# Sums of squares of queries and keys: squares as the moving operand of four column tiles, a row copy and a turn, and norms taken later in the slot

## The chip, the cores and the metric

One core of one Trainium2 chip runs the kernel. The metric is the time on the device of one launch, in microseconds (us), as the median of several runs. The kernel's own names for the engines are used beside the usual ones: PE (TensorE, matrix products), DVE (VectorE), ACT (ScalarE), POOL (GpSimd), SP (SyncE, which here only starts transfers).

## The reference

The input x is 16 sequences of 512 positions by 128 features. A gated linear attention with 8 heads of 128 is followed by a layer norm, a mixture of experts and a second layer norm. The part that matters here:

```python
def _l2norm(u, eps=1e-12):
    n = jnp.sqrt(jnp.sum(u * u, axis=-1, keepdims=True))
    return u / jnp.maximum(n, eps)
...
q = _l2norm((x @ Wq).reshape(Bb, Tt, H, DK))
k = _l2norm((x @ Wk).reshape(Bb, Tt, H, DK))
v = (x @ Wv).reshape(Bb, Tt, H, DV)
alpha = jax.nn.sigmoid(x @ Wg).reshape(Bb, Tt, H, DK)

def step(S, qkva):
    q_t, k_t, v_t, a_t = qkva
    S = a_t[..., None] * S + k_t[..., None] * v_t[:, :, None, :]
    o_t = jnp.einsum('bhkv,bhk->bhv', S, q_t)
    return (S, o_t)
```

So each query and each key of each head is divided by its own length. That length is a sum over the 128 features.

## The kernel before, in words

The attention runs in 64 slots: 16 sequences times 4 pairs of heads (`P` counts slots, `p` is the pair within a sequence, `par = p % 2` picks one of two sets of buffers). In slot `P` the engines do three things interleaved: the scores of slot P in levels (`scores(par, P, j)` for j = 1, 3, 4, 5, 6, 7; level 6 joins halves of 32 positions, and level 7 halves of 64), the projections and norms of slot P + 1, and the states and outputs of slot P - 1. 63 slots have a next slot. After the slots the experts run ("the second half" below); the change does not touch them.

Queries and keys lie transposed: features on the 128 partitions, positions along a row, 512 per head. A sum over features is therefore a sum over partitions, which PE does by a product with ones. The way of a norm before the change:

- ACT squares the projected rows into `sq_sb` (`square`, line 940), 4 rows of 512 for the 2 heads times q and k.
- PE's `sums_of_squares(P, i)` (line 540) runs twice in a slot, i = 0 for the queries and i = 1 for the keys. Each time it takes 32 blocks of 32 positions as the stationary operand, with a single column of ones moving past it. A sum comes out with positions on partitions, in 8 columns.
- DVE's `clamp_sums` (line 1261) moves the 8 columns to `ss_sb`, POOL's `inverse_norms` (line 445) raises them to the power -0.5 into `rn_sb`.
- For the queries PE's `spread_norms` (line 560) turns each column back into rows by 8 transposes, and DVE's `normalise_q` (line 1177) multiplies the queries by them. For the keys ACT scales the values by the inverse norm (`take_values`, line 958).

Each engine works through its own instructions strictly in the order in which the program lists them, and waits at an instruction until the semaphores named before it have reached a count. The order around the change is written out by hand in each engine's `body`. DVE's levels are the loop `for j in range(3, 7)`: after the scores of level j it multiplies the decays into the queries and the keys (`grow`, line 1205), keeps the level's scores (`keep_level`, line 1225) and multiplies up the decay totals (`block_product`, line 304). PE's level j + 1 waits for DVE's `grow` of level j:

```python
pe.wait_ge(k_up, P * 6 + j - 2)
pe.wait_ge(q_up, P * 6 + j - 2)
```

and `spread_norms` waits for the first power of POOL:

```python
pe.wait_ge(rn_done, P * 2 + 1)
```

POOL's `norms` takes, in this order, the power of the queries' sums, a product of decays of 512 elements (`block_product` 0), the power of the keys' sums, and a product of 256 elements.

Of the kernel before, what the change touches and what calls it, by code (L numbers as in the profile page):

```python
# [5 lines left out]
def gated_linear_attention_and_moe_block(  # L6
# [58 lines left out]
    C = 128  # L65
# [19 lines left out]
    with ctx:  # L85
# [52 lines left out]
        s_sb = sb("s_sb", [128, HP, NC - 1, D])  # L138
        ss_sb = sb("ss_sb", [128, 16])
# [80 lines left out]
        xt_evac = sem("xt_evac")  # L220
        ss_full = sem("ss_full")
# [216 lines left out]
        def _(pool):  # L438
# [4 lines left out]
            def norms(par, P):  # L443

                def inverse_norms(i):

                    pool.wait_ge(ss_evac, P * 2 + i + 1)
                    nc.gpsimd.tensor_tensor(rn_sb[par][:, i, :, :].rearrange("p h c -> p (h c)"), ss_sb[:, i * G:(i + 1) * G],  # L448
                                            expo[:, 0:G], ALU.pow).then_inc(rn_done, 1)

                inverse_norms(0)

                await_count(pool, q1_done, (P - 1) * 3)
                await_count(pool, k_up, (P - 1) * 6)
                await_count(pool, q_up, (P - 1) * 6)
                await_count(pool, s_done, (P - 1) * HP * (NC - 1))
                block_product(pool, nc.gpsimd, par, P, 0)
                inverse_norms(1)
                block_product(pool, nc.gpsimd, par, P, 1)
# [40 lines left out]
        def _(pe):  # L500
# [39 lines left out]
            def sums_of_squares(P, i, n_x):  # L540

                pe.wait_ge(sq_full, P * 4 + (i + 1) * HP)
                if i == 0:

                    pe.wait_ge(xt_evac, n_x)
                    pe.wait_ge(x_lo, n_x)
                    await_count(pe, qn_done, P * HP)
                else:

                    await_count(pe, s_done, (P - 1) * HP * (NC - 1))  # L550
                for h in range(HP):
                    for c in range(NC):
                        col = h * NC + c
                        for n in range(NB):
                            lo = c * C + n * SB
                            mm = nc.tensor.matmul((nb_ps, su_ps)[i][n * SB:(n + 1) * SB, col:col + 1],  # L556
                                                  sq_sb[:, i * HP + h, lo:lo + SB], ones_wide[:, 0:1], start=True, stop=True)
                mm.then_inc(ss_full, 1)
# [67 lines left out]
            def state_updates(par, P, h):  # L626

                pe.wait_ge(kt_evac, P * HP + h + 1)
                pe.wait_ge(pj_evac, (P + 1) * 8)
                if h == 0:  # L630

                    await_count(pe, s_done, P * HP * (NC - 1))
                    pe.wait_ge(ss_evac, 2 * (P + 1))
                for c in range(NC - 1):
                    mm = nc.tensor.matmul((su_ps, kt_ps)[h][:, c * D:(c + 1) * D], kt_sb[:, h, c, :],  # L635
                                          v_sb[par][:, c, h * D:(h + 1) * D], start=True, stop=True)
                mm.then_inc(su_full, 1)
# [55 lines left out]
            sums_of_squares(0, 0, 1)  # L693
# [18 lines left out]
            sums_of_squares(0, 1, 1)  # L712
# [5 lines left out]
            def body(b, first=False, last=False):  # L718
                for p, P, has_prev, has_next in slots(b, first, last):
# [25 lines left out]
                    if has_next:  # L745
                        project(next_p, P + 1, wk, 3)
                        sums_of_squares(P + 1, 0, n_x)
# [3 lines left out]
                    if has_next:  # L751
                        project(next_p, P + 1, wg, 4)
                        project(next_p, P + 1, wg, 5)
                    scores(par, P, 5)
                    if has_prev:
                        outputs_of_state(prev_p, P - 1, 0)
                    if has_next:
                        sums_of_squares(P + 1, 1, n_x)
                        spread_norms(1 - par, P + 1)
                    scores(par, P, 6)  # L760
# [161 lines left out]
        def _(act):  # L922
# [17 lines left out]
            def square(par, P, n):  # L940

                act.wait_ge(pj_evac, P * 8 + n + 1)
                await_count(act, ss_full, (P - 1) * 2 + n // HP + 1)
# [3 lines left out]
            def take_gate(par, P):  # L947
                for h in range(HP):
# [7 lines left out]
                    nc.scalar.activation(a_sb[par][:, h * T:(h + 1) * T], pj[h][:, :], ACT.Sigmoid).then_inc(pj_evac, 1)  # L956

# [71 lines left out]
            take_gate(0, 0)  # L1029
            for n in range(2):  # L1030
# [8 lines left out]
            def body(b, first=False, last=False):  # L1039
                for p, P, has_prev, has_next in slots(b, first, last):  # L1040
# [18 lines left out]
                    if has_next:  # L1059
                        take_tile(1 - par, P + 1, 3)  # L1060
                        square(1 - par, P + 1, 3)
                        take_gate(1 - par, P + 1)
# [113 lines left out]
        def _(dve):  # L1176
# [84 lines left out]
            def clamp_sums(P, i):  # L1261
                dve.wait_ge(ss_full, P * 2 + i + 1)
                await_count(dve, rn_done, (P - 1) * 2 + i + 1)
                nc.vector.tensor_scalar(ss_sb[:, i * G:(i + 1) * G], (nb_ps, su_ps)[i][:, 0:G], L2_EPS * L2_EPS, None,  # L1264
                                        ALU.max).then_inc(ss_evac, 1)
# [60 lines left out]
            clamp_sums(0, 0)  # L1326

# [6 lines left out]
            clamp_sums(0, 1)  # L1334
# [13 lines left out]
            def body(b, first=False, last=False):  # L1348
                for p, P, has_prev, has_next in slots(b, first, last):
# [9 lines left out]
                    for j in range(3, 7):  # L1359
                        if j == 6 and has_next:  # L1360
                            for h in range(HP):
                                normalise_q(1 - par, P + 1, h)

# [16 lines left out]
                        if j == 3 and has_next:  # L1380
                            clamp_sums(P + 1, 0)
# [11 lines left out]
                        if j == 5 and has_next:  # L1393
                            clamp_sums(P + 1, 1)
                    if has_next:
                        own_products(1 - par, P + 1)
# [200 lines left out]
```

## Time and profile before

| | us |
|---|---|
| median of 3 runs | 1863.56 |
| lowest and highest run | 1863.16, 1868.34 |
| the profiled execution, its own time | 1872.54 |
| its span, first to last instruction | 1870.8 |
| PE busy | 1754.8 (94%) |
| PE weight loads busy (beside the products) | 1406.0 (75%) |
| DVE busy | 1461.4 (78%) |
| ACT busy | 1077.9 (58%) |
| POOL busy | 601.4 (32%) |

The span is read against the busy times: the engine with the largest share is the first candidate for what bounds the kernel, and the waits tell whether it stands for others. Matmuls overlap in the engine, so a group of many short ones is read by where the next group starts, not by the sum of their durations. "issue" as the reason of a wait means that the engine waited for nothing that the profile records.

### The profile page before, as it was taken

Reading aid. Unit: us, or ns where it says so; the run is one execution under the profiler, and the core shown is the slowest. Engines: PE = TensorE matmul, PEld = TensorE weight load, DVE = VectorE, ACT = ScalarE, POOL = GpSimd, SP = SyncE. Lnnn points to the kernel's source line nnn. Section 1 sums busy time; section 2 is a strip of 40 time slices with the busy share of each in tenths; the row PEclk is TensorE's granted clock in tenths of the full one; section 3 lists DMA queues with packets and bytes.
Section 4 is the critical chain, followed back from the end, with each engine's and each line's share of the span. In section 5 each row is a group of like instructions: output and inputs, shape, how many; then the busy total and the mean of one; then the engine's idle time right before and its main releaser. Section 6 shows DMA issues by size and latency. Waiting matters only on the chain.

```text
span 1870.8 us, 81894 instructions
## 1 busy us (share of the span) xinstructions
PE 1754.8 (94%) x35719; PEld 1406.0 (75%) x35719; DVE 1461.4 (78%) x3391; ACT 1077.9 (58%) x2352; POOL 601.4 (32%) x474
## 2 busy tenths in 40 slices
PE   6999999999999999999999999999799999999997
PEld 5777887878888787777888877778666666666664
DVE  5878888887887888787877878788668787878785
ACT  5665565656566556555665665556365555555553
POOL 4222322322322222232222322232134444444443
PEclk9999999999999999999999999999999999999999
DMA  7000000000000000000000000000000000000000
GB/s 209 4 9 9 4 9 4 9 5 8 9 4 9 4 9 9 4 9 3 9 4 9 4 9 9 4 9 4 8 6 23 12 23 12 23 12 23 12 17 12
DMA packets 28657, 26.99 MB, mean 14 GB/s; under 512 B 1928, under 2 KB 23696, under 8 KB 28304
## 3 DMA queue, kind: packets, MB, share of 16 engines
q1 hardware_dynamic: 28304, 21.77, 3.9%
q8 instruction: 284, 4.65, 1.0%
q14 instruction: 69, 0.57, 0.1%
HBM read 13.38 MB, written 4.19 MB: 9 GB/s over the span
## 4 chain that ended last, share of the span: by engine, by line
PE 78%; DVE 10%; issue 7%; ACT 4%; DMA 0%; POOL 0%; DVEq 0%; POOLq 0%; SPq 0%; ACTq 0%
PE bank L516 11%; PE bank L518 9%; PE bank L517 9%; PE bank L649 8%; PE bank L604 7%; PE bank L659 5%; PE bank L635 5%; PE bank L607 5%; PE bank L556 5%; PE bank L566 4%; PE bank L623 3%; PE bank L592 2%; ACT v_sb L967 2%; DVE v_sb L1508 2%; PE bank L834 1%
## 5 line engine op out<-in xcount | busy, mean ns | idle before, releaser
L448 POOL TENSOR_TENSOR rn_sb<-ss_sb,expo 128x8 f32<-128x8 f32 x128 | 213.5, 1668 | 776.9 <-DVE ss_sb L1264 776.9
L1219 DVE TENSOR_TENSOR qq_sb<-qq_sb,tot_sb 128x512 f32<-128x512 f32 (+1 forms) x384 | 262.9, 685 | 192.9 <-PE bank L604 150.0
L1219 DVE TENSOR_TENSOR k_sb<-k_sb,tot_sb 128x512 f32<-128x512 f32 (+1 forms) x384 | 323.5, 842 | 6.0 <-PE bank L607 5.9
L992 ACT ACTIVATE at_sb<-diag_sb 32x256 f32<-32x256 f32 x256 | 106.0, 414 | 169.7 <-DVE diag_sb L1231 165.0
L967 ACT ACTIVATE v_sb<-bank,rn_sb 128x128 f32<-128x128 f32 x512 | 139.1, 383 | 81.5 <-PE bank L518 78.7
L604 PEld LDWEIGHTS bank<-qq_sb,k_sb 128*32 128x32 f32 x12288 | 128.3, 110 | 59.2 <-issue 45.0
L604 PE MATMUL bank<-qq_sb,k_sb 128*32 128x16 f32 x12288 | 149.0, 185 | 23.1 <-issue 21.5
L956 ACT ACTIVATE a_sb<-bank 128x512 f32<-128x512 f32 x128 | 76.4, 598 | 159.2 <-PE bank L518 153.1
L649 PE MATMUL bank<-v_sb,at_sb 128*128 128x128 f32 x1024 | 153.0, 293 | 5.3 <-DVE res L1271 2.9
L1108 ACT ACTIVATE sq_sb<-bank 128x512 f32<-128x512 f32 x160 | 95.6, 598 | 101.0 <-PE bank L518 99.7
L484 POOL TENSOR_TENSOR wq_lo<-v_sb,wq_hi 128x512 fp32r<-128x512 f32 x80 | 103.9, 1299 | 145.5 <-ACT wq_hi L1115 145.5
L516 PE MATMUL bank<-wg_hi,ew_hi 128*128 128x512 f32 x320 | 140.3, 438 | 7.0 <-DVE v_sb L1508 7.0
L484 POOL TENSOR_TENSOR wk_lo<-v_sb,wk_hi 128x512 fp32r<-128x512 f32 x80 | 104.0, 1300 | 131.7 <-ACT wk_hi L1115 131.7
L314 POOL TENSOR_TENSOR tot_sb<-a_sb 128x512 f32<-128x512 f32 x64 | 89.9, 1405 | 165.9 <-ACT a_sb L956 127.4
L649 PEld LDWEIGHTS bank<-v_sb,at_sb 128*128 128x128 f32 x1024 | 128.4, 196 | 10.7 <-issue 6.3
L607 PE MATMUL bank<-qq_sb,k_sb 128*32 128x32 f32 (+1 forms) x3072 | 121.6, 209 | 7.5 <-issue 6.6
L607 PEld LDWEIGHTS bank<-qq_sb,k_sb 128*32 128x32 f32 (+1 forms) x3072 | 105.0, 123 | 29.5 <-issue 16.3
L517 PE MATMUL bank<-wg_lo,ew_hi 128*128 128x512 f32 x320 | 126.2, 395 | 0.0
L518 PE MATMUL bank<-wg_hi,ew_lo 128*128 128x512 f32 x320 | 125.5, 392 | 0.0
L556 PEld LDWEIGHTS bank<-ones_wide,sq_sb 128*32 128x32 f32 x8192 | 82.8, 111 | 53.1 <-issue 43.8
L659 PE MATMUL bank<-s_sb,qq_sb 128*128 128x128 f32 x768 | 113.1, 283 | 3.4 <-DVE s_sb L1257 2.6
L556 PE MATMUL bank<-ones_wide,sq_sb 128*32 128x1 f32 x8192 | 95.7, 172 | 20.1 <-issue 18.5
(198 smaller groups left out, 4358.0 us busy)
## 6 DMA issues: line engine op xcount, KB each, us to landing
x_nat<-in_L_attn_x_dram SPq DMA_DIRECT2D x16, 256.0 KB, 3.6
x_nat<-x_all SPq DMA_DIRECT2D x16, 256.0 KB, 2.4
out_dram<-k_sb SPq DMA_DIRECT2D x16, 256.0 KB, 2.3
ew_raw<-in_L_ffn_exp_w_dram SPq DMA_DIRECT2D x3, 512.0 KB, 5.3
qq_sb<-in_L_attn_Wq_dram SPq DMA_DIRECT2D x1, 512.0 KB, 3.8
qq_sb<-in_L_attn_Wk_dram SPq DMA_DIRECT2D x1, 512.0 KB, 5.7
k_sb<-in_L_attn_Wg_dram SPq DMA_DIRECT2D x1, 512.0 KB, 6.5
k_sb<-in_L_attn_Wv_dram SPq DMA_DIRECT2D x1, 512.0 KB
```

The lines of the kernel that those rows point to most:

```text
L448: nc.gpsimd.tensor_tensor(rn_sb[par][:, i, :, :].rearrange("p h c -> p (h c)"), ss_sb[:, i * G:(i + 1) * G], expo[:, 0:G], ALU.pow).then_i ...
L484: nc.gpsimd.tensor_tensor(gc_part[1][(par * NE + e) % 4], gc[(par * NE + e) % 4], gc_part[0][(par * NE + e) % 4].bitcast(fp32), ALU.subtra ...
L516: nc.tensor.matmul(out_ap, stat(0), mov(0), start=start, stop=False)
L517: nc.tensor.matmul(out_ap, stat(0), mov(1), start=False, stop=False)
L518: return nc.tensor.matmul(out_ap, stat(1), mov(0), start=False, stop=stop)
L556: mm = nc.tensor.matmul((nb_ps, su_ps)[i][n * SB:(n + 1) * SB, col:col + 1], sq_sb[:, i * HP + h, lo:lo + SB], ones_wide[:, 0:1], start=Tr ...
L604: mm = nc.tensor.matmul(out[n * SB:(n + 1) * SB, g * HB:(g + 1) * HB], k_sb[par][:, left:left + SB], halves(qd_sb[par][:, left:left + SB], ...
L607: mm = nc.tensor.matmul(out[2 * m * n:2 * m * n + m, g * m:(g + 1) * m], k_sb[par][:, left:left + m], qd_sb[par][:, left + m:left + 2 * m] ...
L649: nc.tensor.matmul(y_ps[:, c * D:(c + 1) * D], at_sb[par][:, h * NC + c, :], v_sb[par][:, c, h * D:(h + 1) * D], start=p == 0 and h == 0 a ...
L659: mm = nc.tensor.matmul(y_ps[:, c * D:(c + 1) * D], qd_sb[par][:, lo:lo + C], s_sb[:, h, c - 1, :], start=False, stop=p == NP - 1 and h == ...
L967: last = nc.scalar.activation(v_sb[par][:, c, h * D:(h + 1) * D], pj[n][:, at:at + D], ACT.Copy, scale=rn_sb[par][:, 1, h, c:c + 1])
L1219: return nc.vector.tensor_tensor(view, view, by, ALU.mult)
```

## The change

The squares of q and k are now summed in one go. The ones are the stationary operand, 32 columns wide, and the squares move past them, 512 positions at a time. The four rows (2 of q, 2 of k) go to the four groups of 32 columns of the array, so that each sum comes out as a row over the positions, repeated over 32 partitions (`sums_of_squares(P, n_x)`). ACT copies that bank to `ss_row` (`take_sums`), PE transposes it in 4 blocks of 128 (`turn_sums`), and DVE picks 16 columns out of it in one instruction (`clamp_sums(P)`). The products with ones move behind `scores(4)` and the chunk outputs of the first head; the turn stands behind `scores(5)`; `spread_norms` stands behind `scores(6)`. POOL takes both powers behind its first product of decays. DVE scales the queries behind its level 6.

```diff
+        ss_row = sb("ss_row", [128, T])
...
                 def inverse_norms(i):
 
-                    pool.wait_ge(ss_evac, P * 2 + i + 1)
+                    pool.wait_ge(ss_evac, P + 1)
...
-                inverse_norms(0)
...
                 block_product(pool, nc.gpsimd, par, P, 0)
+                inverse_norms(0)
                 inverse_norms(1)
                 block_product(pool, nc.gpsimd, par, P, 1)
...
-            def sums_of_squares(P, i, n_x):
-
-                pe.wait_ge(sq_full, P * 4 + (i + 1) * HP)
-                if i == 0:
-
-                    pe.wait_ge(xt_evac, n_x)
-                    pe.wait_ge(x_lo, n_x)
-                    await_count(pe, qn_done, P * HP)
-                else:
-
-                    await_count(pe, s_done, (P - 1) * HP * (NC - 1))
-                for h in range(HP):
-                    for c in range(NC):
-                        col = h * NC + c
-                        for n in range(NB):
-                            lo = c * C + n * SB
-                            mm = nc.tensor.matmul((nb_ps, su_ps)[i][n * SB:(n + 1) * SB, col:col + 1],
-                                                  sq_sb[:, i * HP + h, lo:lo + SB], ones_wide[:, 0:1], start=True, stop=True)
+            def sums_of_squares(P, n_x):
+
+                pe.wait_ge(sq_full, (P + 1) * 2 * HP)
+                pe.wait_ge(xt_evac, n_x)
+                pe.wait_ge(x_lo, n_x)
+                await_count(pe, qn_done, P * HP)
+                for t in range(2 * HP):
+                    mm = nc.tensor.matmul(nb_ps[t * SB:(t + 1) * SB, :], ones_wide[:, 0:SB], sq_sb[:, t, :], start=True, stop=True)
+                mm.then_inc(sr_full, 1)
+
+            def turn_sums(P):
+
+                pe.wait_ge(sr_evac, P + 1)
+                await_count(pe, s_done, (P - 1) * HP * (NC - 1))
+                for c in range(NC):
+                    mm = nc.tensor.transpose(su_ps[:, c * C:(c + 1) * C], ss_row[:, c * C:(c + 1) * C], ident[:, :])
                 mm.then_inc(ss_full, 1)
...
                         project(next_p, P + 1, wk, 3)
-                        sums_of_squares(P + 1, 0, n_x)
                     scores(par, P, 4)
                     if has_prev:
                         outputs_of_chunk(prev_p, P - 1, b if p else b - 1, 0)
                     if has_next:
+                        sums_of_squares(P + 1, n_x)
                         project(next_p, P + 1, wg, 4)
                         project(next_p, P + 1, wg, 5)
                     scores(par, P, 5)
+                    if has_next:
+                        turn_sums(P + 1)
                     if has_prev:
                         outputs_of_state(prev_p, P - 1, 0)
+                    scores(par, P, 6)
                     if has_next:
-                        sums_of_squares(P + 1, 1, n_x)
                         spread_norms(1 - par, P + 1)
-                    scores(par, P, 6)
...
+            def take_sums(P):
+
+                act.wait_ge(sr_full, P + 1)
+                await_count(act, ss_full, P)
+                nc.scalar.activation(ss_row[:, :], nb_ps[:, :], ACT.Copy).then_inc(sr_evac, 1)
...
                         square(1 - par, P + 1, 3)
+                        take_sums(P + 1)
                         take_gate(1 - par, P + 1)
...
+            def clamp_sums(P):
+                dve.wait_ge(ss_full, P + 1)
+                await_count(dve, rn_done, P * 2)
+                nc.vector.tensor_scalar(ss_sb[:, :].rearrange("p (t c) -> p t c", c=NC),
+                                        su_ps[:, :].rearrange("p (c t r) -> p t c r", t=2 * HP, r=SB)[:, :, :, 0],
+                                        L2_EPS * L2_EPS, None, ALU.max).then_inc(ss_evac, 1)
...
                     for j in range(3, 7):
-                        if j == 6 and has_next:
-                            for h in range(HP):
-                                normalise_q(1 - par, P + 1, h)
-
...
-                        if j == 3 and has_next:
-                            clamp_sums(P + 1, 0)
...
                         if j == 5 and has_next:
-                            clamp_sums(P + 1, 1)
+                            clamp_sums(P + 1)
                     if has_next:
+                        for h in range(HP):
+                            normalise_q(1 - par, P + 1, h)
                         own_products(1 - par, P + 1)
```

PE from level 5 of the scores to the chunk outputs of the second head, in the slot P = 1, before the change. L604 and L607 are the scores, L659 the state outputs, L556 the sums of the keys, L566 `spread_norms`, L649 the chunk outputs:

```order
L604 MATMUL bank<-qq_sb,k_sb 32x16 [waits q_up,k_up,sc_evac]
L604 MATMUL bank<-qq_sb,k_sb 32x16 x31
L659 MATMUL bank<-s_sb,qq_sb 128x128 [waits q_up,s_done]
L659 MATMUL bank<-s_sb,qq_sb 128x128 x2
L556 MATMUL bank<-ones_wide,sq_sb 32x1 [waits s_done,sq_full]
L556 MATMUL bank<-ones_wide,sq_sb 32x1 x31
L566 MATMUL bank<-ident,rn_sb 128x128 [waits s_done,rn_done]
L566 MATMUL bank<-ident,rn_sb 128x128 x7
L607 MATMUL bank<-qq_sb,k_sb 32x32 [waits q_up,k_up,sc_evac]
L607 MATMUL bank<-qq_sb,k_sb 32x32 x15
L649 MATMUL bank<-v_sb,at_sb 128x128 [waits pj_evac,sc_act,at_diag]
```

The same place of the changed kernel (L557 is `turn_sums`; the other groups keep their numbers there):

```order
L604 MATMUL bank<-qq_sb,k_sb 32x16 [waits q_up,k_up,sc_evac]
L604 MATMUL bank<-qq_sb,k_sb 32x16 x31
L557 MATMUL bank<-ident,ss_row 128x128 [waits s_done,sr_evac]
L557 MATMUL bank<-ident,ss_row 128x128 x3
L659 MATMUL bank<-s_sb,qq_sb 128x128 [waits q_up,s_done]
L659 MATMUL bank<-s_sb,qq_sb 128x128 x2
L607 MATMUL bank<-qq_sb,k_sb 32x32 [waits q_up,k_up,sc_evac]
L607 MATMUL bank<-qq_sb,k_sb 32x32 x15
L566 MATMUL bank<-ident,rn_sb 128x128 [waits s_done,rn_done]
L566 MATMUL bank<-ident,rn_sb 128x128 x7
L649 MATMUL bank<-v_sb,at_sb 128x128 [waits pj_evac,sc_act,at_diag]
```

The 32 small products left this place, 4 transposes came, and the 8 transposes of the norms went behind the scores of level 6.

POOL in two consecutive slots before the change (L448 is the power, L314 a product of decays):

```order
L448 TENSOR_TENSOR rn_sb<-ss_sb,expo 128x8 [waits ss_evac]
L314 TENSOR_TENSOR tot_sb<-a_sb 128x512 [waits s_done,q_up,pj_evac,k_up,q1_done]
L448 TENSOR_TENSOR rn_sb<-ss_sb,expo 128x8 [waits ss_evac]
L314 TENSOR_TENSOR tot_sb<-tot_sb 128x256 [waits tot_pool]
L448 TENSOR_TENSOR rn_sb<-ss_sb,expo 128x8 [waits ss_evac]
```

And of the changed kernel (L451 and L317 are the same two operations):

```order
L317 TENSOR_TENSOR tot_sb<-a_sb 128x512 [waits s_done,q_up,pj_evac,k_up,q1_done]
L451 TENSOR_TENSOR rn_sb<-ss_sb,expo 128x8 [waits ss_evac] x2
L317 TENSOR_TENSOR tot_sb<-tot_sb 128x256 [waits tot_pool]
L317 TENSOR_TENSOR tot_sb<-a_sb 128x512 [waits s_done,q_up,pj_evac,k_up,q1_done]
L451 TENSOR_TENSOR rn_sb<-ss_sb,expo 128x8 [waits ss_evac] x2
```

The power of the queries' sums stood ahead of the large product of decays; now both powers stand behind it.

## Rows read from the trace of the kernel before

**Rows 1.** The page: shares of the chain that ended last.
```profile
PE 78%; DVE 10%; issue 7%; ACT 4%; DMA 0%; POOL 0%; DVEq 0%; POOLq 0%; SPq 0%; ACTq 0%
```

**Rows 2.** Busy times in the stretch of the slots: us, then each engine (instructions).
```profile
60.00:1300.00 1240.00, 1183.26 (x31690) 999.21 (x31690) 997.26 (x2368) 736.18 (x1764) 342.69 (x256) 0.99 0.03 7
```

**Rows 3.** What PE waited for, 60 to 1300 us: us in total, times, longest.
```profile
PE bank L604 <- issue: 17.3, 27, 1.2
PE bank L556 <- issue: 16.9, 21, 1.3
PE bank L607 <- issue: 6.2, 19, 0.8
...
PE bank L566 <- issue: 2.7, 2, 1.7
```

**Rows 4.** PE timeline, one slot: start, duration, instruction, [idle before].
```profile
1003.28 0.71 PE L556 MATMUL bank<-ones_wide,sq_sb 128*32 128x1 f32 x64
1003.88 0.44 PE L604 MATMUL bank<-qq_sb,k_sb 128*32 128x16 f32 x31
...
1006.35 0.39 PE L517 MATMUL bank<-xT_lo,wg_hi 128*128 128x512 f32 x1
1006.58 0.40 PE L518 MATMUL bank<-xT_hi,wg_lo 128*128 128x512 f32 x1
...
1007.60 0.74 PE L604 MATMUL bank<-qq_sb,k_sb 128*32 128x16 f32 x64
1008.26 0.94 PE L659 MATMUL bank<-s_sb,qq_sb 128*128 128x128 f32 x6
1009.13 0.71 PE L556 MATMUL bank<-ones_wide,sq_sb 128*32 128x1 f32 x64
1009.77 1.09 PE L566 MATMUL bank<-ident,rn_sb 128*128 128x128 f32 x8
1010.79 0.70 PE L607 MATMUL bank<-qq_sb,k_sb 128*32 128x32 f32 x32
1011.42 1.16 PE L649 MATMUL bank<-v_sb,at_sb 128*128 128x128 f32 x8
...
1015.66 0.43 PE L580 MATMUL bank<-e_sb,ones_wide 128*32 128x128 f32 x8
1016.02 0.50 PE L516 MATMUL bank<-xT_hi,wq_hi 128*128 128x512 f32 x1
```

**Rows 5.** DVE, POOL and ACT timelines of the same slot.
```profile
1008.44 0.69 DVE L1219 TENSOR_TENSOR qq_sb<-qq_sb,tot_sb 128x512 f32<-128x512 f32 x1 [0.46 <-issue]
1009.05 1.53 DVE L1219 TENSOR_TENSOR k_sb<-k_sb,tot_sb 128x512 f32<-128x512 f32 x1
...
1011.21 0.17 DVE L1264 TENSOR_SCALAR ss_sb<-bank 128x8 f32<-128x8 f32 x1
...
1008.47 1.56 POOL L314 TENSOR_TENSOR tot_sb<-a_sb 128x512 f32<-128x512 f32 x1 [2.53 <-ACT a_sb L956]
1011.46 1.64 POOL L448 TENSOR_TENSOR rn_sb<-ss_sb,expo 128x8 f32<-128x8 f32 x1 [1.42 <-DVE ss_sb L1264]
...
1007.01 1.29 ACT L956 ACTIVATE a_sb<-bank 128x512 f32<-128x512 f32 x2 [2.36 <-PE bank L518]
```

**Rows 6.** PE and POOL timelines of a slot with p = 1.
```profile
963.57 0.74 PE L604 MATMUL bank<-qq_sb,k_sb 128*32 128x16 f32 x64
...
966.94 0.24 PE L556 MATMUL bank<-ones_wide,sq_sb 128*32 128x1 f32 x7 [0.94 <-issue]
...
968.20 1.64 POOL L448 TENSOR_TENSOR rn_sb<-ss_sb,expo 128x8 f32<-128x8 f32 x1 [2.19 <-DVE ss_sb L1264]
```

**Rows 7.** Busy times around that pause; the third number from the right is the granted clock.
```profile
967.18:970.59 3.41, 3.41 (x44) 3.02 (x44) 2.66 (x12) 1.73 (x6) 2.39 (x3) 0.50 0.02 5
```

**Rows 8.** PE timeline of gate projections at the lower clock.
```profile
1211.36 0.63 PE L518 MATMUL bank<-xT_hi,wg_lo 128*128 128x512 f32 x1
1211.79 0.63 PE L516 MATMUL bank<-xT_hi,wg_hi 128*128 128x512 f32 x1
```

More of the change, by code:

```diff
@@ L220, in gated_linear_attention_and_moe_block @@
         xt_evac = sem("xt_evac")
+        sr_full = sem("sr_full")
+        sr_evac = sem("sr_evac")
         ss_full = sem("ss_full")
@@ L632, in state_updates @@
                     await_count(pe, s_done, P * HP * (NC - 1))
-                    pe.wait_ge(ss_evac, 2 * (P + 1))
+                    pe.wait_ge(ss_evac, P + 1)
                 for c in range(NC - 1):
@@ L692, in _ @@
             mm.then_inc(fold_pe, 1)
-            sums_of_squares(0, 0, 1)
+            sums_of_squares(0, 1)
             pe.wait_ge(fold_sb, 4)
@@ L709, in _ @@
             pe.wait_ge(fold_bias, 1)
-            sums_of_squares(0, 1, 1)
+            turn_sums(0)
             spread_norms(0, 0)
@@ L942, in square @@
                 act.wait_ge(pj_evac, P * 8 + n + 1)
-                await_count(act, ss_full, (P - 1) * 2 + n // HP + 1)
+                await_count(act, sr_full, P)
                 src = (q_sb, k_sb)[n // HP][par][:, (n % HP) * T:(n % HP + 1) * T]
@@ L1029, in _ @@
             take_gate(0, 0)
+            take_sums(0)
             for n in range(2):
@@ L1259, in states @@
                                                        op0=ALU.mult, op1=ALU.add).then_inc(s_done, 1)
[L1261 to L1265, printed above, removed]
+            def clamp_sums(P):
[4 more added lines that the diff above has]
+                                        L2_EPS * L2_EPS, None, ALU.max).then_inc(ss_evac, 1)
             def ln_halves(n, y, resid):
@@ L1325, in _ @@
             nc.vector.tensor_tensor(swf_b[:, :], swi_b[:, :], sc[1][:, 0:4], ALU.add).then_inc(fold_bias, 1)
-            clamp_sums(0, 0)
             for n in range(2):
@@ L1333, in _ @@
             nc.vector.tensor_tensor(swf[1][:, :], sc[0][:, :], swf[0][:, :].bitcast(fp32), ALU.subtract).then_inc(w_lo, 1)
-            clamp_sums(0, 1)
+            clamp_sums(0)
             dve.wait_ge(const_dve, 5)
```

## Prediction

> **What bounds the kernel now.** I read the chain that ended last first: PE holds 78% of it, DVE 10%, and 7% is time in which an engine waited for nothing that is recorded [rows 1]. Then the busy times of the stretch that holds nearly all slots, 60 to 1300 us: PE is busy 1183.26 of 1240 us, which leaves 56.7 us idle, against 243 us for DVE and 504 us for ACT [rows 2]. The list of what PE waited for says that even this little is hardly a wait for another engine: the large entries are all "issue", 17.3 us ahead of the scores L604 and 16.9 us ahead of the sums L556 [rows 3]. So in the slots PE is the bound. A slot is 20 us (1240 us hold 62 of them), PE stands 0.9 us of it, and whatever is put on PE, or makes PE stand, lengthens the slot one for one unless something gives way.
>
> The timeline shows how narrow the cover is. From the start of the state outputs L659 at 1008.26 to the chunk outputs L649 at 1011.42 PE works without a hole through L659, L556, L566 and L607 [rows 4]. In the same 3.16 us DVE grinds through level 5: it scales the queries from 1008.44, the keys from 1009.05 for 1.53 us (ended 1010.58), and the scores of level 6 start on PE at 1010.79, just behind it [rows 4, 5]. The sums and the norms' transposes are what fills PE while DVE does that. DVE's clamp starts at 1011.21 and POOL's power runs from 1011.46 for 1.64 us, to 1013.10 [rows 5]; nobody on PE waits for that one now, since it is the keys' norm and only the copies of the values use it. The power of the queries was taken long before.
>
> **The change, part by part.**
>
> *The new wait.* PE's `spread_norms` waits for the first power. That power now follows the one clamp, which follows DVE's level 5, where the second clamp already stood. So its end can be read off the present trace: 1013.10, in a slot whose level 5 scores started at 1007.60, 5.50 us earlier [rows 4, 5]. On PE the turn (half of the eight transposes, which take 1.02 us to the next group, so 0.46 without the switch at their end), L659 (0.87 to the next group) and the level 6 scores (0.63) stand ahead of it, some 2.0 us of work from 1008.26 on; first PE waits about 1 us for DVE's keys ahead of level 6, then nearly 2 us for the power. With 0.05 us for the signal (POOL followed DVE's clamp by 0.08) and 0.92 for the eight transposes, L649 starts at 1014.07, where it started at 1011.42: plus 2.65 us. Queued behind the waiting transposes is everything on PE: both outputs, the values, level 7, the next slot. In the slots with p = 1 DVE has the layer norm's variance ahead of the clamp: there the power ends at 969.84, 6.27 us after level 5 began at 963.57, so 0.77 us later [rows 6]. There are 15 such slots. 63 x 2.65 + 15 x 0.77 = **+179 us**.
>
> POOL's large product does not come into it: 1008.47 to 1010.03 ends before the clamp [rows 5]. The second power ends 1.64 us later than the first; it releases the values' copies on ACT at about 1014.8, when PE has only reached the values' products, so it is hidden.
>
> *The sums.* One group of 32 old ones took 0.60 us of PE (1003.28 to 1003.88); the second group is inside the stretch above. For the new ones the nearest row is L580, four products with ones in the same four column tiles, 128 positions wide: 0.36 us from its start to the next group [rows 4]. If the tiles did not run side by side that would be eight passes of 0.114 us, 0.91 us, so they do. Two passes of 0.114 are 0.23 and the rest, 0.13, is fixed. At 512 wide: 4 x 0.23 + 0.13 = 1.05 us, and 0.1 for one more switch between wide and narrow tiles; less 0.60 is 0.55. Bounds: 0.26 if only a pass rate of 0.107 counts and no switch is added, 0.9 if all of 0.36 grows fourfold. I take 0.48, near the low side since the fixed part overlaps: 63 x 0.48 = **+30 us**.
>
> The Trainium skill (TensorEngine Tiling (Array Packing), Instruction Overhead) has about 60 cycles for each matmul, so that one column costs as much as 60. By it, as an estimate, the 64 records of a group would take 1.6 us at 2.4 GHz, not 0.60, and the removed work would be worth 2 us more in a slot. The row of 0.60 us decides against it; the sum goes by the row.
>
> *Idle time given back.* PE's "issue" stops ahead of L556, L607 and L566 (25.8 us together [rows 3]) fall mostly in the stretch that will now be set by DVE and POOL, where they are absorbed, with a few more at its edges: I take 30. A slot has 1022 PE records (31690 products and as many loads in 62 slots [rows 2]); 256 go and 24 come, so there are 23% fewer, and PE pauses anyway. Of the other 27 us idle I give back 12. **-42 us.** Bounds 0 and -57.
>
> *ACT, DVE.* The added copy is like ACT's other copies of 128x512, half of the 1.29 us pair, and falls into the 2.36 us in which ACT waits for the gate projection [rows 5]: nothing. If PE were ready earlier it would cost 0.6. DVE loses a clamp (0.17) and gets queries' scaling behind level 6. After the norms are spread it has six operations of 0.61 us (1008.44 to 1009.05), ending near 1017.7; PE wants them for the next slot's first scores, 4.6 us (1011.42 to 1016.02) plus a projection of 0.9 after L649, at about 1019.6. Hidden with 1.9 us to spare.
>
> *PE's clock.* In the p = 1 slot shown PE stood 0.94 us ahead of the last sums (records 1.11 us apart), and right behind it, from 967.18 to 970.59, the granted clock was 0.50, the 1.2 GHz level [rows 6, 7]. Of 18 such pauses of 1.1 us or more between matmul starts within the slots, 9 were followed by such a fall. At that level a projection's pass took 0.43 us (1211.36 to 1211.79) where 0.23 is usual (1006.35 to 1006.58) [rows 4, 8], so 3.41 us of it cost up to 1.6 us, and 1.4 when part is spent on small work. The new pauses, 1 us and 2 us with only the small level 6 scores between, are worse than those 18. I take two slots in three, 42, less the 9 there are: 33 x 1.4 = **+46 us**. Bounds: -13 (it never falls) and +76 (in every slot).
>
> The Trainium skill (TensorE: Matmul & The Clock Gate, HAM oscillation) describes a kernel that falls and recovers in every iteration of its loop because of a wait in each. By that the fall would come in all 63 slots, +76 instead of +46; the 9 of 18 here leave it open.
>
> *The start.* Ahead of the first values the chain now has the copy, the turn, the product of decays and a power in a row, 0.6 + 0.5 + 1.56 + 1.64, some of it already there: **+4 us**.
>
> Sum: 179 + 30 - 42 + 46 + 4 = +217 us, on the profiled execution's own 1872.5 us (span 1870.8 and 1.7 around it): 2090. The median of the runs, 1863.56, is 9 us below that execution, so I expect a median of 2081; leaning a little to the side of the more absorbed idle time, **2077 us**.
>
> **Rivals.**
>
> *The clock stays up.* For: half of the present pauses did nothing. Against: the pauses are longer and in each slot. 217 - 46 - 13 = 158, time 2022.
>
> *It falls in each slot, and the idle time stays.* 217 + 30 + 42 = +289, time 2150; with only the first, 2110.
>
> *The four column tiles do not run side by side at 512 wide,* so that the sums do not do what they are for. Against: L580. Eight passes of 0.456 are 3.65 us, 2.5 more than taken: +158, time 2235.
>
> *Not slower: it is the number of instructions that sets PE's pace.* The stops are "issue", the code is long, and 23% fewer records in a 20 us slot would be worth 4.6 us if PE's time went by their number, 290 us in all, against 183 for the new wait and the start: 107 us faster, time 1757. It decides from 2.9 us a slot on. Against: the groups at issue here run at 0.60 us for 128 records, 1.2 us a slot altogether, and wide passes of 0.23 us fill most of the rest, whose time does not hang on the number of records; the stops themselves are 0.9 us a slot.
>
> **How the numbers follow.** Forecast 0.72, clock stays up 0.12, each slot with idle kept 0.08, tiles in series 0.04, not slower 0.04 (0.03 faster, 0.01 within 0.3%, which is about what a measurement of this kernel can tell from no change). The range takes in the clock's two ends, and the sums' and idle time's inner part: 2020 to 2128.
>
> **What would show it.** Right: in the profile after, `spread_norms` waits about 2 us in each slot, for POOL's power; L607 waits about 1 us for DVE's keys; DVE and POOL show the same 5.5 us from level 5's start to the power's end; the slot is near 23.4 us; PE's clock row has many short falls; the four wide products take about 1 us to the next group. Wrong, if the power's end comes much sooner after level 5 (DVE's keys at 0.7 instead of 1.53 us, because POOL's product no longer meets them), if PE's idle share is still under 6%, or if the slots are set by something that the pauses uncover, such as DVE's chain behind the norms.

## The result and the profile after

| | before | changed |
|---|---|---|
| median, us | 1865.95 (4 runs, 1863.16 to 1871.16) | 2088.63 (4 runs, 2088.06 to 2089.49) |
| span of the profiled execution, us | 1870.8 | 2087.1 |
| PE busy | 94% | 87% |
| mean granted clock of PE | 0.986 | 0.947 |

The changed kernel takes 1.119 times the time of the kernel before (95% interval 1.116 to 1.121), 223 us more. The forecast was 2077 us, its range 2020 to 2128.

The chain that ended last, from the page of the changed kernel, answers to [rows 1]:

```profile
PE 62%; DVE 19%; issue 9%; POOL 5%; ACT 3%; DMA 0%; DVEq 0%; POOLq 0%; SPq 0%; ACTq 0%
PE bank L518 10%; PE bank L519 8%; PE bank L520 7%; PE bank L649 7%; POOL rn_sb L451 5%; DVE k_sb L1228 5%; PE bank L566 5%; PE bank L635 4%; PE bank L604 4%; PE bank L549 3%; PE bank L659 3%; PE bank L623 3%; PE bank L607 3%; DVE qq_sb L1228 2%; PE bank L592 2%
```

POOL had no share in it; now its power `rn_sb` stands in it with 5%, and DVE's scaling of the keys `k_sb` with 5%. The busy times of the slots, and what PE waited for in them (us in total, times, longest us), answer to [rows 2, 3]:

```profile
60.00:1500.00 1440.00, 1243.73 (x24700) 1017.34 (x24699) 989.97 (x2299) 772.18 (x1825) 341.38 (x254) 0.94 0.02 5
```

```profile
PE bank L566 <- POOL rn_sb L451: 122.7, 60, 3.1
PE bank L607 <- issue: 65.4, 60, 1.1
PE bank L649 <- DVE res L1281: 4.8, 15, 0.3
PE bank L518 <- issue: 2.2, 14, 0.2
```

In each of 60 slots PE stands 1.09 us ahead of the level 6 scores and then for POOL's power, 2.05 us on average: 1.77 us in most slots and about 2.95 us in the 15 slots with p = 1. The wait of 1.09 us is labelled "issue" since the profile found no releaser; what ends it is DVE's scaling of the keys, as the timelines of one slot and the end of the slot ahead of it show (PE, then DVE and POOL; they answer to [rows 4, 5]):

```profile
980.63 1.09 PE L566 MATMUL bank<-ident,rn_sb 128*128 128x128 f32 x8 [1.77 <-POOL rn_sb L451]
981.55 1.06 PE L649 MATMUL bank<-v_sb,at_sb 128*128 128x128 f32 x8
...
992.88 0.73 PE L604 MATMUL bank<-qq_sb,k_sb 128*32 128x16 f32 x64
993.53 1.16 PE L649 MATMUL bank<-v_sb,at_sb 128*128 128x128 f32 x8
994.62 1.06 PE L549 MATMUL bank<-sq_sb,ones_wide 128*32 128x512 f32 x8
...
997.21 0.74 PE L604 MATMUL bank<-qq_sb,k_sb 128*32 128x16 f32 x64
997.87 0.66 PE L557 MATMUL bank<-ident,ss_row 128*128 128x128 f32 x4
998.37 0.83 PE L659 MATMUL bank<-s_sb,qq_sb 128*128 128x128 f32 x6
1000.29 0.70 PE L607 MATMUL bank<-qq_sb,k_sb 128*32 128x32 f32 x32 [1.09 <-issue]
...
1002.76 1.41 PE L566 MATMUL bank<-ident,rn_sb 128*128 128x128 f32 x8 [1.77 <-POOL rn_sb L451]
1003.96 1.91 PE L649 MATMUL bank<-v_sb,at_sb 128*128 128x128 f32 x8
```

```profile
998.66 1.53 DVE L1228 TENSOR_TENSOR k_sb<-k_sb,tot_sb 128x512 f32<-128x512 f32 x1
...
1000.82 0.17 DVE L1273 TENSOR_SCALAR ss_sb<-bank 128x16 f32<-128x16 f32 x1
1001.27 0.69 DVE L1228 TENSOR_TENSOR qq_sb<-qq_sb,tot_sb 128x512 f32<-128x512 f32 x1 [0.28 <-PE bank L607]
1001.88 0.69 DVE L1228 TENSOR_TENSOR k_sb<-k_sb,tot_sb 128x512 f32<-128x512 f32 x1
...
998.08 1.56 POOL L317 TENSOR_TENSOR tot_sb<-a_sb 128x512 f32<-128x512 f32 x1 [15.32 <-ACT a_sb L957]
1001.07 3.24 POOL L451 TENSOR_TENSOR rn_sb<-ss_sb,expo 128x8 f32<-128x8 f32 x2 [1.43 <-DVE ss_sb L1273]
```

The keys end at 1000.19 and level 6 starts at 1000.29. The clamp starts at 1000.82; the first of the two powers (half of 3.24 us) ends near 1002.7 and the transposes start at 1002.76, 5.55 us after level 5 began.

At 1003.96 L649 takes 1.91 us instead of 1.16. The busy times of that moment show why (the third number from the right is the granted clock):

```profile
1003.40:1006.80 3.40, 3.40 (x19) 3.40 (x17) 2.67 (x4) 0.00 (x0) 1.49 (x2) 0.50 0.00 0
```

The clock fell to 0.50, the 1.2 GHz level, behind the two pauses. Counted over the slots of the trace, PE spent 191 us at that level in 34 stretches (22 of them 6.83 us long, 12 of them 3.41), against 31 us in 9 before.

### The profile page after: what moved, and what is told of

Its sections match the earlier page's. It is cut to its first block, busy times and chain, and to the rows that moved or that the text cites. A ratio compares the mean times of both kernels' runs of the same rounds, so it can differ in the third digit from the quotient of the medians.

```text
span 2087.1 us, 67046 instructions
## 1 busy us (share of the span) xinstructions
PE 1822.5 (87%) x28295; PEld 1428.5 (68%) x28295; DVE 1453.8 (70%) x3327; ACT 1116.0 (53%) x2416; POOL 600.5 (29%) x474
## 4 chain that ended last, share of the span: by engine, by line
PE 62%; DVE 19%; issue 9%; POOL 5%; ACT 3%; DMA 0%; DVEq 0%; POOLq 0%; SPq 0%; ACTq 0%
PE bank L518 10%; PE bank L519 8%; PE bank L520 7%; PE bank L649 7%; POOL rn_sb L451 5%; DVE k_sb L1228 5%; PE bank L566 5%; PE bank L635 4%; PE bank L604 4%; PE bank L549 3%; PE bank L659 3%; PE bank L623 3%; PE bank L607 3%; DVE qq_sb L1228 2%; PE bank L592 2%
## 5 line engine op out<-in xcount | busy, mean ns | idle before, releaser
L317 POOL TENSOR_TENSOR tot_sb<-a_sb 128x512 f32<-128x512 f32 x64 | 98.7, 1542 | 1053.4 <-ACT a_sb L957 1053.4
L1228 DVE TENSOR_TENSOR k_sb<-k_sb,tot_sb 128x512 f32<-128x512 f32 (+1 forms) x384 | 307.2, 800 | 68.6 <-PE bank L607 68.6
L451 POOL TENSOR_TENSOR rn_sb<-ss_sb,expo 128x8 f32<-128x8 f32 x128 | 213.2, 1683 | 103.1 <-DVE ss_sb L1273 103.1
L566 PE MATMUL bank<-ident,rn_sb 128*128 128x128 f32 x512 | 97.4, 352 | 131.2 <-POOL rn_sb L451 131.2
L607 PE MATMUL bank<-qq_sb,k_sb 128*32 128x32 f32 (+1 forms) x3072 | 118.4, 206 | 70.0 <-issue 67.6
L649 PE MATMUL bank<-v_sb,at_sb 128*128 128x128 f32 x1024 | 168.5, 317 | 4.8 <-DVE res L1281 4.8
L566 PEld LDWEIGHTS bank<-ident,rn_sb 128*128 128x128 f32 x512 | 76.4, 178 | 138.5 <-POOL rn_sb L451 138.5
L607 PEld LDWEIGHTS bank<-qq_sb,k_sb 128*32 128x32 f32 (+1 forms) x3072 | 104.3, 121 | 88.9 <-issue 80.6
L604 PEld LDWEIGHTS bank<-qq_sb,k_sb 128*32 128x32 f32 x12288 | 123.2, 110 | 56.9 <-issue 49.3
L649 PEld LDWEIGHTS bank<-v_sb,at_sb 128*128 128x128 f32 x1024 | 151.9, 227 | 7.3 <-issue 5.8
L1189 DVE TENSOR_TENSOR qq_sb<-qq_sb,bank 128x512 f32<-128x512 f32 x128 | 85.4, 686 | 94.8 <-PE bank L566 94.7
L518 PE MATMUL bank<-wg_hi,ew_hi 128*128 128x512 f32 x320 | 140.4, 439 | 6.4 <-DVE v_sb L1512 6.4
L604 PE MATMUL bank<-qq_sb,k_sb 128*32 128x16 f32 x12288 | 141.2, 185 | 2.6 <-DVE k_sb L1228 1.7
L659 PE MATMUL bank<-s_sb,qq_sb 128*128 128x128 f32 x768 | 123.5, 304 | 0.9 <-DVE s_sb L1266 0.9
```

The source lines that it names most:

```text
L518: nc.tensor.matmul(out_ap, stat(0), mov(0), start=start, stop=False)
L566: mm = nc.tensor.transpose(bank[:, c * C:(c + 1) * C], rn_sb[par][:, 0, h, c:c + 1].to_broadcast([128, 128]), ident[:, :])
L604: mm = nc.tensor.matmul(out[n * SB:(n + 1) * SB, g * HB:(g + 1) * HB], k_sb[par][:, left:left + SB], halves(qd_sb[par][:, left:left + SB], ...
L607: mm = nc.tensor.matmul(out[2 * m * n:2 * m * n + m, g * m:(g + 1) * m], k_sb[par][:, left:left + m], qd_sb[par][:, left + m:left + 2 * m] ...
L649: nc.tensor.matmul(y_ps[:, c * D:(c + 1) * D], at_sb[par][:, h * NC + c, :], v_sb[par][:, c, h * D:(h + 1) * D], start=p == 0 and h == 0 a ...
L659: mm = nc.tensor.matmul(y_ps[:, c * D:(c + 1) * D], qd_sb[par][:, lo:lo + C], s_sb[:, h, c - 1, :], start=False, stop=p == NP - 1 and h == ...
```

## The experiments

The kernel before ran beside each: its median was 1858.23 us beside the first four and 1872.19 us beside the last three, which ran on another chip. So a difference between an experiment of the first group and one of the second is uncertain by that shift of 14 us; the ratios to the kernel before do not have it.

**1. The norms' transposes without the wait.**

```diff
-                pe.wait_ge(rn_done, P * 2 + 1)
...
-                                                 rn_sb[par][:, 0, h, c:c + 1].to_broadcast([128, 128]), ident[:, :])
+                                                 expo[:, c:c + 1].to_broadcast([128, 128]), ident[:, :])
```

> The changed kernel, but the eight transposes of the norms read a constant tile instead of the norms, so they no longer wait for GpSimd's power; every other instruction stays (the queries are scaled by a constant instead of their norms). Theory A (the new wait for the power is the main cost): the 2.05 us that TensorE stands ahead of the transposes in each of the 63 slots (about 129 us) go, and with the shorter pause most of the falls of the granted clock (about 60 us more), so about 1900 to 1930 us. Rival B (the instruction mix is the cost and the pause only moves): the pause turns up at the level 6 scores or the outputs, and the time stays above 2040 us.

Measured: 1890.45 us, 198 us less than the changed kernel, a little beyond the expected side. The wait ahead of the transposes is gone, and about 11 us of it came back at other places (the waits for ACT at L591 and L518):

```profile
PE bank L606 <- issue: 65.4, 60, 1.1
PE bank L591 <- ACT at_sb L1010: 7.1, 14, 0.5
...
PE bank L518 <- ACT v_sb L973: 4.1, 14, 0.4
```

The pause for the keys is still there to the last tenth, and the granted clock is 1.00 in the slots. So the pause of 1.09 us, alone, did not pull the clock down in any slot. This fells the rival that the pause only moves.

**2. The order alone, with the narrow sums.** The kernel before, changed in these places only:

```diff
-                inverse_norms(0)
                 await_count(pool, q1_done, (P - 1) * 3)
...
                 block_product(pool, nc.gpsimd, par, P, 0)
+                inverse_norms(0)
                 inverse_norms(1)
...
                         sums_of_squares(P + 1, 1, n_x)
-                        spread_norms(1 - par, P + 1)
                     scores(par, P, 6)
+                    if has_next:
+                        spread_norms(1 - par, P + 1)
...
-                        if j == 6 and has_next:
-                            for h in range(HP):
-                                normalise_q(1 - par, P + 1, h)
...
-                        if j == 3 and has_next:
-                            clamp_sums(P + 1, 0)
...
                         if j == 5 and has_next:
+                            clamp_sums(P + 1, 0)
                             clamp_sums(P + 1, 1)
                     if has_next:
+                        for h in range(HP):
+                            normalise_q(1 - par, P + 1, h)
                         own_products(1 - par, P + 1)
```

> The kernel before, with its narrow sums left where they were; only the order changes: both clamps behind level 5, both powers behind GpSimd's large product, the norms' transposes behind the level 6 scores, the queries' scaling behind level 6. Theory A (the order costs): the power ends about 5.6 us after level 5 starts, as in the changed kernel, TensorE pauses about 2 us ahead of the norms' transposes, and the time is 2050 to 2100 us. Rival B (the wide sums, the copy and the turn cost): under 1920 us. The issue stops: if their going is due to the pauses they are gone here too; if it is due to fewer instructions, most of 48 us stay.

Measured: 2092.83 us, 1.125 times the kernel before (1.123 to 1.128). The order alone costs as much as the whole change, the low clock with it: 242 us in 57 stretches of the slots. What PE waited for, 60 to 1300 us, 52 slots:

```profile
PE bank L565 <- POOL rn_sb L448: 101.2, 52, 3.1
PE bank L606 <- issue: 25.0, 35, 0.8
PE bank L603 <- issue: 12.7, 21, 1.3
PE bank L555 <- issue: 10.5, 18, 1.0
```

The stops ahead of the small scores and the narrow sums (L603 and L555 here, L604 and L556 before) are still there: 0.45 us a slot, where [rows 3] give 0.55. Pauses alone hardly remove these two.

**3. The pauses filled.**

```diff
+                    if has_next:
+                        for n in range(1):
+                            nc.tensor.matmul(nb_ps[:, :], ident[:, :], sq_sb[:, 0, :], start=True, stop=True)
                     scores(par, P, 6)
                     if has_next:
+                        for n in range(2):
+                            nc.tensor.matmul(nb_ps[:, :], ident[:, :], sq_sb[:, 0, :], start=True, stop=True)
                         spread_norms(1 - par, P + 1)
```

> The changed kernel with three extra products of 128x512 in each slot that nobody reads, one ahead of the level 6 scores (into the 1.1 us pause) and two ahead of the norms' transposes (into the 2 us pause). Theory C (the low clock costs, beside the waits): the granted clock stays at 1.0 in the slots and the time falls by 50 to 80 us, to 2010 to 2040 us, though TensorE does 2.6 us more work in each slot. Rival (the low clock falls into time that is idle anyway, or the extra products do not fit the pauses): 2080 to 2130 us.

Measured: 2010.53 us, 78 us less than the changed kernel, by adding work. The extra products do not hold the slot up: from level 5 to the chunk outputs the slots take 6.47 to 6.48 us (7.65 with p = 1), and in the changed kernel, where the clock stays up, 6.47 to 6.48 as well. Busy times of the slots:

```profile
60.00:1300.00 1240.00, 1206.82 (x22645) 905.53 (x22644) 892.25 (x2086) 697.95 (x1649) 319.40 (x233) 1.00 0.02 6
```

PE is busy for 97% of the stretch and the clock stays at 1.00. So the 78 us are what the low clock cost in the changed kernel: 1.2 us a slot.

**4. Wide sums, early norms.** The changed kernel, with the turn in the bank of the sums:

```diff
                 block_product(pool, nc.gpsimd, par, P, 0)
-                inverse_norms(0)
...
+                inverse_norms(0)
                 await_count(pool, q1_done, (P - 1) * 3)
...
-                await_count(pe, s_done, (P - 1) * HP * (NC - 1))
...
-                    mm = nc.tensor.transpose(su_ps[:, c * C:(c + 1) * C], ss_row[:, c * C:(c + 1) * C], ident[:, :])
+                    mm = nc.tensor.transpose(nb_ps[:, c * C:(c + 1) * C], ss_row[:, c * C:(c + 1) * C], ident[:, :])
...
                         project(next_p, P + 1, wg, 5)
+                        turn_sums(P + 1)
                     scores(par, P, 5)
-                    if has_next:
-                        turn_sums(P + 1)
                     if has_prev:
                         outputs_of_state(prev_p, P - 1, 0)
-                    scores(par, P, 6)
                     if has_next:
                         spread_norms(1 - par, P + 1)
+                    scores(par, P, 6)
...
                         if j == 4 and has_prev:
                             states(1 - par, P - 1)
+                        if j == 4 and has_next:
+                            clamp_sums(P + 1)
...
-                        if j == 5 and has_next:
-                            clamp_sums(P + 1)
```

`normalise_q` is back ahead of DVE's level 6.

> The changed kernel's wide sums, row copy and turn, but with the norms early: the turn goes into the bank of the sums and stands ahead of the level 5 scores, the clamp behind level 4's states, the first power ahead of GpSimd's large product, the norms' transposes and the queries' scaling where the kernel before has them. Theory A (order is the whole loss, the wide sums are nearly neutral on TensorE and take issue stops away): no pause for the power, the granted clock as in the kernel before, sums and turn 1.6 us a slot instead of 1.2 (plus 23 us), issue stops down from 48 us to under 20: 1835 to 1860 us, a little faster than the kernel before. Rival B (the wide sums themselves are slow): over 1900 us.

Measured: 1857.21 us, 0.9985 times the kernel before (0.9976 to 0.9995). The loss is gone with the order. What is left is no gain to speak of, at the far end of what was expected. PE's waits, 60 to 1300 us:

```profile
PE bank L566 <- POOL rn_sb L451: 28.0, 62, 0.5
PE bank L519 <- issue: 5.0, 15, 0.3
PE bank L649 <- DVE res L1280: 4.7, 15, 0.3
```

The "issue" stops fell from 48 us to 5. The sums' 256 small records a slot are what left, so the stops hang on those groups; whether on their number or on where they stood, no run separates. But the power now ends 0.45 us after PE wants it, in each of 62 slots: 28 us.

**5. Both powers ahead of the large product.** The changed kernel, one thing moved on POOL:

```diff
+                inverse_norms(0)
+                inverse_norms(1)
                 await_count(pool, q1_done, (P - 1) * 3)
...
                 block_product(pool, nc.gpsimd, par, P, 0)
-                inverse_norms(0)
-                inverse_norms(1)
```

> The changed kernel with one thing moved: on GpSimd both powers stand ahead of the large product of decays instead of behind it. Theory D (VectorE's scaling of the keys in level 5 takes 1.53 us instead of 0.69 because GpSimd's large product runs at the same time, and this chain sets the slot): with the product gone from there, the keys take 0.69 us, TensorE's pause ahead of the level 6 scores falls from 1.1 to about 0.3 us, the clamp and the power come 0.84 us earlier, and the time falls by 63 x 0.84 = 53 us and somewhat more for the clock, to 2020 to 2040 us. Rival (the 1.53 us belong to the instruction or its access pattern): 2080 to 2095 us.

Measured: 2028.27 us, 60 us less than the changed kernel, where 53 and somewhat more were expected. In its timelines (DVE, PE, POOL) the keys are scaled in 0.69 us instead of 1.53, level 6 waits 0.25 us instead of 1.09, and the product itself, behind the powers, takes 1.04 us instead of 1.56:

```profile
1007.75 0.69 DVE L1228 TENSOR_TENSOR k_sb<-k_sb,tot_sb 128x512 f32<-128x512 f32 x1
```

```profile
1006.30 0.73 PE L604 MATMUL bank<-qq_sb,k_sb 128*32 128x16 f32 x64
...
1008.54 0.70 PE L607 MATMUL bank<-qq_sb,k_sb 128*32 128x32 f32 x32 [0.25 <-issue]
```

```profile
1009.32 3.24 POOL L451 TENSOR_TENSOR rn_sb<-ss_sb,expo 128x8 f32<-128x8 f32 x2 [16.35 <-DVE ss_sb L1273]
1012.52 1.04 POOL L317 TENSOR_TENSOR tot_sb<-a_sb 128x512 f32<-128x512 f32 x1
```

So the 1.53 us are two engines in each other's way, not the instruction.

The wait for the keys is nearly gone, the one for the power is as long as before (1.77 us, about 2.95 with p = 1), and the granted clock still fell: 157 us at the 1.2 GHz level, in 46 stretches of 3.41 us, instead of 191. What PE waited for, 60 to 1300 us:

```profile
PE bank L566 <- POOL rn_sb L451: 111.1, 54, 3.1
PE bank L607 <- issue: 13.3, 54, 0.2
```

So the long pause is enough for a fall, without the one of 1.09 us.

The Trainium skill (SBUF — State Buffer, SBUF: two separate sides) says that a VectorE operation with two SBUF inputs and a GpSimd operation that reads SBUF share a pair of ports as an exclusive lock, held for a whole instruction. The product and the keys agree with it: in the changed kernel the product starts with the queries' scaling (998.08 and 998.05), ends at 999.64, and the keys end 0.55 us later. The 0.84 us that DVE loses are less than the 1.04 us of a whole product, which fits a product that had begun before the keys; the exact split no run shows. The power does not agree: it reads two SBUF tiles for about 1.62 us, and DVE's scalings at 1001.27 and 1001.88, inside it, took their usual 0.69 us. So did all 111 scalings of 128x512 that lay inside a power of the changed kernel (0.68 to 0.72 us). Here the measurement decides: a power can stand beside DVE's scalings, a large product costs them time.

**6. The turn earlier, and both powers first.** Experiment 4, and:

```diff
                 inverse_norms(0)
+                inverse_norms(1)
...
                 block_product(pool, nc.gpsimd, par, P, 0)
-                inverse_norms(1)
...
                         project(next_p, P + 1, wg, 4)
+                        turn_sums(P + 1)
                         project(next_p, P + 1, wg, 5)
-                        turn_sums(P + 1)
```

> The version with wide sums and early norms, with two more moves: the turn stands between the two gate projections (0.7 us earlier) and both powers stand ahead of the large product on GpSimd. Theory (its 0.45 us pause ahead of the norms' transposes in each slot is the power's end, and what holds it up next, VectorE's keys, is not stretched since the product runs later): the pause goes, 62 x 0.45 = 28 us, so about 1829 us, 1.5% faster than the kernel before. Rival (the copy of the row is not done when the turn comes, or the product now stretches something on the path): 1850 to 1865 us.

Measured: 1835.33 us, 0.981 times the kernel before (0.979 to 0.983): 22 us under experiment 4, where 28 were expected (by the ratios it is 1.75%, or 33 us; the two ran on different chips). It beats both kernels. What PE waited for:

```profile
PE bank L607 <- DVE k_sb L1227: 14.5, 15, 1.0
PE bank L649 <- DVE res L1280: 5.0, 15, 0.6
PE bank L519 <- issue: 4.8, 15, 0.3
```

The wait for the power is gone. In its place level 6 waits for the keys, 1 us in each of 15 slots, 14.5 us that the expectation did not have.

**7. The turn earlier alone.** Experiment 6 with POOL's order of experiment 4.

> As the previous one, but only the turn moves; GpSimd keeps power, large product, power, small product. Theory D: the product then starts about 0.8 us earlier, meets VectorE's keys of level 5 again (about 1.5 us instead of 0.69), and the level 6 scores wait for them, so the gain of the turn is lost: 1850 to 1875 us. Rival (no stretch): 1829 us like the previous one.

Measured: 1861.28 us, 0.994 times the kernel before (0.992 to 0.997), as theory D had it. POOL's product moves forward into DVE's keys again, in all 63 slots; in experiments 4 and 6 no scaling of the keys took over 1.2 us (PE, DVE, POOL):

```profile
1021.23 0.70 PE L607 MATMUL bank<-qq_sb,k_sb 128*32 128x32 f32 x32 [0.96 <-issue]
```

```profile
1019.60 1.53 DVE L1227 TENSOR_TENSOR k_sb<-k_sb,tot_sb 128x512 f32<-128x512 f32 x1
```

```profile
1019.06 1.52 POOL L317 TENSOR_TENSOR tot_sb<-a_sb 128x512 f32<-128x512 f32 x1
```

Against experiment 6, on the same chip, POOL's order alone costs 26 us. Against experiment 4 the wait for the power (28.0 us) is gone and PE stands 37.5 us ahead of level 6 instead: taking one wait away let an engine off the path start its work sooner, and that cost what had been won.

## Why the prediction was right, and where its sizes were off

**The new wait** (predicted +179 us, about 1 us ahead of level 6 and nearly 2 ahead of the transposes): right in mechanism and place. The waits are 1.09 and 1.77 us, the power ended 5.5 us after level 5 began, as read off the trace before. Experiments 1 and 2 show it from both sides: without the wait 198 us go, with the order alone 235 us come. In an undisturbed slot level 5 to the chunk outputs takes 3.82 us before (1007.60 to 1011.42, [rows 4]). In the slot ahead of the one shown, where the clock was up, the transposes started at 980.63 and L649 at 981.55, so 0.92 us go on top of the 5.55: 6.47, or 2.65 more, the figure of the sum. For the slots with p = 1 it was too small: they take 7.65 us in experiment 3, 1.18 more than the others, not 0.77. That makes this term 182 us.

**The sums** (+30 us, 0.48 a slot): the four column tiles run side by side at 512 wide, too. L549 takes from 1018.74 to 1019.73, 0.99 us to the next group:

```profile
1018.74 1.07 PE L549 MATMUL bank<-sq_sb,ones_wide 128*32 128x512 f32 x8
1019.73 0.50 PE L518 MATMUL bank<-xT_hi,wg_hi 128*128 128x512 f32 x1
```

From L604 to L604 around it, without its stop of 0.42 us, the place took 3.30 us before (1003.88 to 1007.60, [rows 4]); the place with the wide sums takes 4.33 (992.88 to 997.21), and 0.60 of narrow sums left the stretch ahead of it. That is 0.43 a slot, 27 us. The stop, from the timeline of the kernel before:

```profile
1004.74 0.45 PE L604 MATMUL bank<-qq_sb,k_sb 128*32 128x16 f32 x33 [0.42 <-issue]
```

**Idle time given back** (-42 us): too small, and for a reason that was wrong in part. PE idled 56.7 us in 62 slots before; beside the two new waits it idles 8 us in 60 slots now, so about 48 us are gone. Experiments 2 and 4 tell what removed them: the pauses little, the going of the small instructions most. The prediction gave 30 of its 42 us to absorption by the pauses. And more came back than was idle. Averaged over 62 slots, the stretch from level 5 to the chunk outputs takes 4.48 us before and 6.76 in experiment 3, where no clock effect is left: +142 us. The rest of the slot takes 16.05 and 15.94 us: -7, though the wide sums put 27 into it. Together that is +135, and 182 + 27 less the 13 us of the old falls would be 196: 61 us came back, not 42. The 13 us beyond the recorded idle time no run explains.

**The clock** (42 slots of 63, 33 more than before, +46 us): mis-sized. The prediction counted a fall as 3.41 us long; there were fewer falls (34), but 22 of them were twice that. By experiment 3 the low clock costs 78 us, of which the prediction had 59 (42 x 1.4). The cases "stays up" and "in each slot" are both refuted by the trace. The section that the prediction named for the second (Trainium skill, TensorE: Matmul & The Clock Gate, HAM oscillation) tells of a kernel that waits 3 to 5 us for a transfer in each round, longer than either pause here; the prediction did not say so, and what it took from it for pauses of 1 and 2 us does not follow.

**The sum.** From the first group L604 of the first slot to that of the last, slots took 20.55 us on average before and 23.85 after, 3.30 x 63 = 208 us; the first slot's scores start 5.5 us later (4 were predicted), the rest is 3 us. Of the 208, 77 are the clock (experiment 3's slots average 22.63), and 131 the other terms, for which the prediction had 179 + 30 - 42 - 13 = 154. So the waits and the sums were sized well, the idle time that came back was sized some 20 us too small, and the clock 18 us too small. These two nearly cancel, and that the sum of 217 us meets the 216 us between the two spans is luck. Against the median the forecast was 12 us low: it took off 9 us since the profiled execution before lay that much above its median, and the changed kernel's lay 0.3 us above its own; another 4 us were the lean to the low side.

**The rivals.** Tiles in series: refuted by L549. Not slower through fewer instructions: the 43 us of stops that experiment 4 removed, and perhaps the 13 us above, are of its kind, far from the 290 us that it needed. ACT's copy and the second power cost nothing, as argued: in the changed kernel PE waits for neither.

Open is what sets the 15 longer waits of experiment 6 in detail, what the "issue" stops are, and whether the 14 us between the kernel before in the two groups of runs come from the chip alone.

## What to carry to other kernels

A chain of small steps over several engines cost this kernel nothing while it started early enough; put behind the last possible producer it costs, in each iteration, what its latency exceeds the work that is left to cover it. That latency can be read off the old trace before anything is built (5.50 us read, 5.55 found). When moving work between engines, place the latency chain first and the bulk work of the helper engine behind it: experiment 6 differs from the changed kernel in the order and in the bank of the turn, and is 253 us faster. Look also at what an engine off the path will collide with when it starts sooner.

## What was not expected of the hardware

- Useless products in the pauses made the changed kernel 78 us faster, since the granted clock stayed at 1.00. A pause of 1.09 us in each slot (experiment 1) did not lower it, one of 1.77 us (2.95 with p = 1) did, in 46 stretches of 3.41 us (experiment 5); with the pause of 1.09 us ahead of it, it did in 34 stretches, most of them 6.83 us long (the changed kernel). Length alone does not settle it: in the kernel before the clock fell behind a pause of 0.94 us [rows 6, 7].
- VectorE's scaling of 128x512 took 1.53 us beside GpSimd's product of 128x512 and 0.69 us without it; the product took 1.56 and 1.04 us. Beside GpSimd's power of 128x8 the scaling was not slowed (0.68 to 0.72 us).
- PE's unexplained stops (48 us) went when 232 of 1022 PE records of a slot were taken away; pauses alone left most of those ahead of the small scores and sums.
